# Wide products of ones on TensorE during the opening waits of a fused MLP and adapter kernel

## What is computed

```python
# layer 0: D = 512, FF = 2048
scale = cond @ norm_w.T + 1.0
h = x * (scale[:, None, :] * rsqrt(mean(x * x, -1) + 1e-6))
val, gate = split(h @ up_w.T, 2, -1)
h = val * gelu(gate)
y = act_quant(h) @ weight_quant(down_w).T + x
# layer 1: an adapter of width 128 whose weights depend on cond
Wd_b = Wd + 0.1 * (cond @ Wdd.T + bdd);  Wu_b = Wu + 0.1 * (cond @ Wdu.T + bdu)
out = y + relu(y @ Wd_b.T + bd) @ Wu_b.T + bu
```

## Time and profile before

| | us |
|---|---|
| median of 3 executions | 865.9 (865.81 to 866.25) |
| profiled execution | 866.98 |
| its span, first to last instruction | 865.2 |
| TensorE products busy | 846.8 (98%) |
| VectorE busy | 608.4 (70%) |
| ScalarE busy | 389.9 (45%) |
| GpSimd busy | 73.9 (9%) |

### The profile page before, as it was taken

The page is one execution under the profiler, slowest core; times in us unless marked ns, Lnnn a source line. Parts: engine busy times, 40 slices in busy tenths (PEclk is TensorE's granted clock), DMA queues, the critical chain, the costliest instruction groups (busy, mean ns, idle before and its releaser), DMA issues.

```text
span 865.2 us, 11930 instructions
## 1 busy us (share of the span) xinstructions
PE 846.8 (98%) x4026; PEld 373.9 (43%) x4026; DVE 608.4 (70%) x942; ACT 389.9 (45%) x632; POOL 73.9 (9%) x79
## 2 busy tenths in 40 slices
PE   6999999999999999999999999999999999999998
PEld 5334444444444444444444444444444444444443
DVE  5997666888897765547886664658986764445986
ACT  5678776767545542216545543216433332214000
POOL 0453223210200000000200000000200000000100
PEclk9999999999999999999999999999999999999999
DMA  9879988659788876556587674634447443432231
GB/s 347 308 242 306 332 282 306 219 174 325 246 297 303 312 252 219 204 192 206 207 309 240 230 277 144 203 108 137 144 133 223 137 160 119 159 104 85 98 122 73
DMA packets 64283, 183.50 MB, mean 212 GB/s; under 512 B 7008, under 2 KB 8032, under 8 KB 64224
## 3 DMA queue, kind: packets, MB, share of 16 engines
q1 hardware_dynamic: 63936, 182.48, 60.5%
q10 hardware_dynamic: 288, 0.26, 0.1%
HBM read 152.31 MB, written 29.36 MB: 210 GB/s over the span
## 4 chain that ended last, share of the span: by engine, by line
PE 90%; ACT 3%; DVE 3%; DMA 2%; issue 2%; SPq 0%; POOL 0%; ACTq 0%; DVEq 0%; POOLq 0%
PE aux_ps L1114 10%; PE b_ps L1025 9%; PE b_ps L1029 9%; PE b_ps L1027 9%; PE a_ps L1025 6%; PE a_ps L1027 6%; PE a_ps L1029 6%; PE aux_ps L1070 6%; PE aux_ps L1177 3%; PE aux_ps L1168 3%; PE c_ps L1029 3%; PE c_ps L1027 3%; PE c_ps L1025 3%; PE e_ps L1027 3%; PE e_ps L1029 3%; PE e_ps L1025 3%
## 5 line engine op out<-in xcount | busy, mean ns | idle before, releaser
L1513 DVE SCALAR_TENSOR_TENSOR h_ring<-v_sb,unscale,gelu 128x512 f32<-128x512 f32 x63 | 48.4, 768 | 97.7 <-ACT gelu L836 54.8
L812 ACT ACTIVATE b_ps<-a_ps 128x512 f32<-128x512 f32 x63 | 36.7, 582 | 152.7 <-PE a_ps L1029 152.7
L1025 PE MATMUL b_ps<-t_mov,u_l 128*128 128x512 f16 x252 | 95.5, 379 | 1.6 <-DVE c_ps L1474 1.6
L1029 PE MATMUL b_ps<-t_mov,u_l 128*128 128x512 f16 x252 | 95.5, 379 | 0.0
L1027 PE MATMUL b_ps<-t_mov,u_l 128*128 128x512 f16 x252 | 95.5, 379 | 0.0
L1537 DVE TENSOR_TENSOR hmax<-gelu,hmax 128x512 f32<-128x512 f32 x120 | 82.4, 687 | 6.6 <-ACT gelu L842 1.0
L1114 PE MATMUL aux_ps<-h_ring,wq 128*128 128x512 f16 x384 | 84.9, 379 | 0.3
L711 POOL PARTITION_ALL_REDUCE yscale<-hmax x8 | 17.9, 2266 | 603.0 <-DVE hmax L1537 602.3
L842 ACT ACTIVATE gelu<-h_ring 128x512 f32<-128x512 f32 x64 | 40.3, 630 | 53.0 <-DVE h_ring L1523 52.0
L846 ACT ACTIVATE gelu<-h_ring 128x512 f32<-128x512 f32 x64 | 40.3, 630 | 51.1 <-DVE h_ring L1513 51.1
L1523 DVE SCALAR_TENSOR_TENSOR h_ring<-b_ps,unscale,gelu 128x512 f32<-128x512 f32 x64 | 47.9, 749 | 21.7 <-PE b_ps L1029 21.6
(11 more groups left out here) (217 smaller groups left out, 1640.8 us busy)
## 6 DMA issues: line engine op xcount, KB each, us to landing
w_ring<-in_Wdu SPq DMA_DIRECT2D x64, 512.0 KB, 6.2
w_ring<-in_Wdd SPq DMA_DIRECT2D x56, 512.0 KB, 6.9
u_l<-ul_dram SPq DMA_DIRECT2D x48, 512.0 KB, 4.5
u_e<-ue_dram SPq DMA_DIRECT2D x48, 384.0 KB, 3.1
h_ring<-in_up_w SPq DMA_DIRECT2D x16, 512.0 KB, 7.1
x_sb<-in_x SPq DMA_DIRECT2D x8, 1024.0 KB, 8.1
res<-in_down_w SPq DMA_DIRECT2D x16, 512.0 KB, 6.3
ul_dram<-u_l SPq DMA_DIRECT2D x15, 512.0 KB, 7.6
```

Of the source, the lines that this page charges most:

```text
L1025: pe.matmul(ps[:, :], weight(n, p, 0, k), hi, start=fresh and k == 0, stop=False, skip_group_check=True)
L1029: mm = pe.matmul(ps[:, :], weight(n, p, 1, k), hi, start=False, stop=k == 1, skip_group_check=True)
L1513: dve.scalar_tensor_tensor(out=h_slot(n)[:, TB:TS], in0=val[:, :], scalar=unscale[:, s // 2, j:j + 1], in1=gelu2[:, :], op0=ALU.mult, op1= ...
```

## The change

`warm_ones` is the tile `ones` seen as f16, 128 x 256. `warm(count)` issues so many products of 128 x 128 by 128 x 256 into the first half of `c_ps`, with ones as both operands; nothing reads the result. Twenty-six stand ahead of everything else on TensorE, behind the wait for `ones`, which was ahead of `stat(0)` until now. Thirty more stand between the small products of the opening: 8 behind scale, 6 behind `stat1(0)`, 4 each behind `first_powers`, `stat1(1)`, `stat1(2)` and `stat1(3)`. No other engine's code changes.

```diff
         norm_raw = stage[:, 0, :]
+        warm_ones = ones[:, :].bitcast(F16)
...
+            def warm(count):
+
+                for _ in range(count):
+                    pe.matmul(c_ps[:, 0:256], warm_ones[:, 0:P], warm_ones[:, :],
+                              start=True, stop=True)
+
+            pe.wait_ge(s_const, 1)
+            warm(26)
             pe.wait_ge(s_small, 32)
             ps = take("scale", 0)
             for k in range(KD):
                 mm = pe.matmul(ps[:, B * k:B * k + B], norm_raw[:, P * k:P * k + P],
                                cond_sb[:, 0:B], start=True, stop=True)
             mm.then_inc(s_aux, 1)
-            pe.wait_ge(s_const, 1)
+            warm(8)
             stat(0)
             pe.wait_ge(s_const, 3)
             first_bounds()
             stat1(0)
+            warm(6)
             spread_rs(0)
             first_powers()
+            warm(4)
             stat1(1)
+            warm(4)
             bounds(-2)
             stat1(2)
+            warm(4)
             stat1(3)
+            warm(4)
             first_product(a_ps[0], True, False, B11).then_inc(s_p[1], 1)
```

## The result

The changed kernel takes 872.3 us (median of four executions, 870.6 to 874.0) against 866.1 us before: a ratio of 1.0068, with a 95% interval of 1.0043 to 1.0093. It is slower by more than the 0.2%. Twelve more executions later (e1) gave 869.7 us against 866.8 us, 1.0032 (1.0018 to 1.0046); so the loss is there both times, and about 3 us is the better figure for its size. The prediction was 864.5 us, range 863.0 to 866.5 us.

What follows compares the result with a forecast made beforehand. TensorE's work bounds the kernel from 200 us on, VectorE's chain from 16 to 43 us; an earlier start passes to the end. -0.87 - 0.20 - 0.30 = -1.37 us gives 864.5 us by the median, range 863.0 to 866.5 us.

Steps and rivals of the forecast that it cites:

- the clock should be up by then: At the 8 wides behind scale, ending by 10.2 us: upper clock level assumed, so their cost is taken as 0.
- The slow rival: Clock low when small products begin at 9.8 us: +0.8 before spread_rs(0), +2.0 at stat1(3), 868.7 us; 11%.
- -0.87 us for stat(0): At stat(0), from 9.82 us: its eight loads with products take 0.98 us instead of 1.85 us, on the path.
- -0.20 us for first_powers: At TensorE's first_powers, before VectorE's restart: 0.31 us instead of 0.51 us.
- the gate (ident at 11.30 us): Before spread_rs(0): first_bounds waits for ident, ready at 11.30 us; the roots then come 0.87 us earlier, at 13.4 us.
- The wides' own price: Each 256-column wide product on TensorE: 0.11 us at the upper clock level, 0.21 us at the lower.
- The first product at 19.6 us: TensorE behind first_powers, small products and 16 wides: first a_ps product near 19.6 us instead of 21.0 us.
- -0.30 us at 43 us: At 43.23 us: VectorE's 0.30 us wait for ScalarE's T3 disappears because TensorE is early.
- gain of 1.37 us: Whole kernel: the sum of -0.87 (stat(0)), -0.20 (first_powers) and -0.30 us (VectorE's wait at 43 us).
- Weight loads that keep their pace: Rival at stat(0) and first_powers: they gain nothing and 12 wides push stat1(3) late, 866.5 us; 5%.
- Passing on: Behind 43 us: quads 1 to 15 are a VectorE, ScalarE and TensorE ring, and a common shift goes through it.
- The chances: Overall odds: forecast 57%, a third of it beyond -0.2%; faster 17% + 17% = 34%, slower 11%, within 55%.

Runs made afterwards that it cites:

- e1: The changed kernel again with no edit, twelve executions: 869.7 us against 866.8 us before, ratio 1.0032.
- e11: Against the kernel before: stat1(0) moved ahead of first_bounds; wides 26 at start, 16 behind scale, 8 behind stat(0), 6 behind stat1(0), none behind first_powers; ratio 0.9995.
- e12: e7 once more with no edit; ratio 1.0011 to the kernel before.
- e3: The changed kernel with only the 26 wides at the start and the 8 behind scale, none behind stat(0); ratio 1.0004 to the kernel before.
- e7: The changed kernel with more wides: 26 at start, 16 behind scale, 8 behind stat(0), 6 behind stat1(0), four times 8 on the path; ratio 1.0012 to before.
- e4: The changed kernel without the 26 wides at the start and the 8 behind scale, the 22 later ones kept; ratio 1.0037 to the kernel before.
- e15: e11 with seven of the eight down_w loads in quads 4 to 10 cut to a quarter; ratio 1.0001 to the kernel before.
- e14: e7 with seven of the eight down_w loads in quads 4 to 10 cut to a quarter; ratio 1.0036 to the kernel before.

## Why the prediction was wrong

- **The step that failed** is the level of the clock behind stat(0). The prediction said of the wides ahead of it that "the clock should be up by then", took it to stay up, and priced every small product and every wide from there on at the upper level. The rise itself came about as said, near 6 us. It was gone at 9.4 us, with stat(0) running: the last wide ended at 8.2 us, TensorE was idle for 0.8 us, and 0.5 us of small products had run. Which of the two weighed more isn't separated in this kernel; e11 shows a fall with TensorE busy, and e12 idle time of 1.49 us without one. The slow rival, "the clock is at the lower level when the small products begin", is what happened; it got 11%. The rows had a hint against my choice: the small f32 products from 9.8 to 21 us kept TensorE loaded nearly all the time and did not raise the clock, and I didn't ask whether they would hold it.
- **The slow rival's price** was 2.8 us, from +0.8 at the restart and +2.0 at the stat1 sums. Measured: +0.57 us at the restart, +1.61 us at the stat1 sums, and +0.41 us at spread_rs(1), which it did not name: 2.6 us, less 0.39 us for the early start. The two places were right. Of the +1.07 us from stat(0)'s start to the restart, 0.50 us is not the wides' but the wait for ident behind an early x. It gave 868.7 us, against the 869.7 us of the twelve executions. Why the first four were at 872.3 us is not shown: TensorE waits 1.6 us for w_ring in their profile, and 3.1 us in that of e1.
- **-0.87 us for stat(0)** is nearly right as a duration, wherever the clock was up (1.05 us in e3 and e7 against 1.84 us, so -0.79 us), and -0.20 us for first_powers is right (0.31 us in e7, 13.27 to 13.58 us). It is right on the path only with ident in time: 6.14 to 5.28 us in e7, but 6.98 us in e3 and 6.18 us in e12. The prediction named the gate (ident at 11.30 us) and took it as fixed. It came between 10.9 and 12.3 us in these profiles, and with stat(0) ending at 9.5 to 10.3 us it is what ends last there.
- **The wides' own price** was right: 0.11 us at the upper level (0.88 for eight in e7), 0.21 us at the lower.
- **The first product at 19.6 us** is at 19.62 us in e7, but by luck. In e7 stat(0) starts 1.42 us earlier, and 32 wides stand on the path, not 16. From first_powers' end to the first product the prediction had 4.8 us with 16 wides; e7 has 6.04 us with 32, and so about 4.3 us with 16 (an estimate from 0.11 us each).
- **-0.30 us at 43 us** did not come. In the kernel after the wait is still there (0.29 us), and in e7, where the clock held, it is gone, but VectorE waits 0.39 us for ScalarE at 36.28 us instead, where it had no wait: restart -2.28 us, quad 1 -2.30 us. With the clock held, then, the gain of 1.37 us was 0.86 us at best (e7) and nothing where ident was late (e12).
- **Weight loads that keep their pace** (5%) is out: the small products are nearly all loads and halved their time in e7. The Trainium skill, TensorE: Matmul & The Clock Gate, section LDWEIGHTS (loading the stationary operand), has no clock in the time of a load; the runs disagree with it for f32: 333 ns at the lower level and 192 ns in e3 and e7.
- **Passing on** the shift one to one was near in e4 (3.72 us at quad 1, 3.25 us at quad 16). Over all profiles what quad 16 adds to quad 1 goes from -0.5 to +3.0 us, in steps at quads whose w_ring loads come late, which the prediction didn't put into its range.
- **The chances**: a third of 57% is 19%, where the prediction added 17% to its 34% for faster; nothing hangs on it.

## What to carry to other kernels

A warm-up pays only if what comes behind it also holds the clock; dense small products need not, however busy they keep TensorE. Filler ahead of the path was free here (e3), but filler between steps of the path is priced at the level that you may get, not at the one that you hope for: with 32 wides on the path a held clock was worth 0.6 us at best, within the noise, and a fallen one cost 5 us. Before pricing a faster step, list what else its consumer waits for (here a constant from GpSimd and one more group in the engine's written order), since that is where the gain stops.

## What the runs showed of the hardware

- Small f32 products with 128-column loads did not keep TensorE at the upper level. The clear case is e11, where the clock fell at 15.3 us after 1.8 us of them without a gap (in e15, with the same opening, at 17.9 us); in the kernel after it fell at 9.4 us and in e3 at 10.4 us, with idle time of 0.6 to 0.8 us ahead of the small ones. Eight wides of 0.11 us to every eight small ones held it in 20 of 34 executions (e7, e12, e14).
- f32 weight loads follow the clock: a load of 128 x 128 took 333 ns at the lower level (before) and 192 ns at the upper (e3, e7), and the same eight loads and products 1.84 us and 1.05 us.
- The granted clock of the profile reads 1.00 until its first change, also where the steps of the products show 1.2 GHz (before, e4).
- GpSimd's affine_select on 128 x 128, with nothing in the program to wait for, started between 10.6 and 12.1 us in all profiles, 9.5 us or more after the operation ahead of it (idle for "issue"). Its queue has two MODIFY_POOL_CONFIG entries at 1.1 to 1.2 us, just ahead of it (before, after, e3, e7). What holds it was not tried.
